# A cross attention's tail moved to tokens on rows, and its head loop given the work

## The reference, cut to what matters

```python
x = x + tanh(g_xattn[0]) * L0_xattn(layernorm(x), ctx)
x = x + tanh(g_ffn[0])   * L0_ffn(layernorm(x))
x = x + tanh(g_xattn[1]) * L1_xattn(layernorm(x), ctx, ctx, mask)
x = x + tanh(g_ffn[1])   * L1_ffn(layernorm(x))

def L1_xattn(q, k, v, mask):          # 16 heads of 16, 361 context rows
    qh, kh, vh = heads(q @ w_q.T + b_q), heads(k @ w_k.T + b_k), heads(v @ w_v.T + b_v)
    attn = softmax(where(mask, qh @ kh.T / 4, -inf))
    return merge(attn @ vh) @ w_o.T + b_o

def L1_ffn(xs):                       # 8 experts, hidden 684
    d2 = sum(xs*xs) + sum(centroid*centroid) - 2 * xs @ centroid.T
    w, sel = top_k(sqrt(maximum(d2, 1e-12)), 2); w = softmax(w)
    return sum over the two chosen e of w_e * ((silu(xs @ Wg[e] + bg[e]) * (xs @ W1[e] + b1[e])) @ W2[e] + b2[e])
```

## Time and profile before

| | |
|---|---|
| median of 3 runs | 837.34 us (836.78 to 839.22) |
| the profiled execution's own time | 836.42 us |
| its span, first to last instruction | 834.2 us |
| mean granted TensorE clock | 0.945 of full |
| busy: PE, DVE, ACT, POOL | 745.0, 562.8, 414.6, 241.5 us |
| the chain that ended last: PE, DVE, ACT, POOL | 55%, 14%, 3%, 1% |

### The profile page before, as it was taken

One profiled execution on the slowest core, in us unless ns is written; L12 is line 12 of the kernel. 1 busy time (PEld: TensorE's weight loads), 2 busy tenths in 40 slices (PEclk: granted clock), 3 DMA queues, 4 the chain that ended last, 5 costly groups with the idle time before them and its releaser, 6 DMA issues.

```text
span 834.2 us, 13705 instructions
## 1 busy us (share of the span) xinstructions
PE 745.0 (89%) x4761; PEld 621.0 (74%) x4761; DVE 562.8 (67%) x1030; ACT 414.6 (50%) x896; POOL 241.5 (29%) x195
## 2 busy tenths in 40 slices
PE   6999999999889469989998898888998699999996
PEld 3588888889865168657996566666774699999995
DVE  3369999999728979737666567676554666656652
ACT  4544444443253249835434356565664545655651
POOL 0064544444003514510003302222212133433422
PEclk9999999999999979897999899998789599999999
DMA  6400000000070000000000766545052248999972
GB/s 235 200 2 18 19 19 19 19 1 1 1 279 9 0 0 3 1 1 1 1 9 1 182 158 150 132 108 172 2 195 95 86 163 291 328 304 309 328 227 57
DMA packets 29050, 86.01 MB, mean 103 GB/s; under 512 B 3759, under 2 KB 19599, under 8 KB 25655
## 3 DMA queue, kind: packets, MB, share of 16 engines
q1 hardware_dynamic: 25143, 79.89, 29.1%
q0 software_dynamic: 3840, 5.25, 3.0%
HBM read 74.75 MB, written 10.38 MB: 102 GB/s over the span
## 4 chain that ended last, share of the span: by engine, by line
PE 55%; DVE 14%; issue 4%; ACT 3%; DMA 2%; POOL 1%; POOLq 0%; SPq 0%; DVEq 0%; ACTq 0%
PE PS L490 51%; PE PS L1033 1%; DVE SM L2049 1%; DVE WK L1811 1%; DVE RW L1751 1%; PE PS L662 1%; DVE WK L1808 1%; DMA KST<-mask_rows 1%; DVE RO L1754 1%; PE PS L879 1%; PE PS L1003 1%; ACT SQ L1078 1%; POOL OT L1565 0%; DVE M L2058 0%; DMA out<-YO,TROW 0%
## 5 line engine op out<-in xcount | busy, mean ns | idle before, releaser
L1485 POOL TENSOR_TENSOR PRODL<-RW,PRODH 128x361 fp32r<-128x361 f32 x64 | 64.8, 1016 | 114.7 <-ACT PRODH L1145 111.1
L2049 DVE TENSOR_REDUCE SM<-PS 100x1 f32<-100x362 f32 x128 | 64.9, 531 | 46.5 <-PE PS L490 45.7
L490 PE MATMUL PS<-CTXH,WKV0H 128*128 128x362 f32 x256 | 85.8, 335 | 9.5 <-DVE RW L1707 8.9
L490 PE MATMUL PS<-CTXL,WKV0H 128*128 128x362 f32 x256 | 84.1, 328 | 0.0
L490 PE MATMUL PS<-CTXH,WKV0L 128*128 128x362 f32 x256 | 83.9, 328 | 0.0
L1334 ACT ACTIVATE WK<-PS 120x400 f32<-120x400 f32 (+1 forms) x96 | 48.3, 507 | 43.1 <-PE PS L490 42.2
L490 PEld LDWEIGHTS PS<-CTXH,WKV0H 128*128 128x128 f32 x256 | 48.3, 188 | 15.9 <-DVE RW L1707 11.0
L490 PE MATMUL PS<-KST,QST 97*100 97x362 f32 x128 | 54.4, 437 | 5.9 <-DMA KST<-mask_rows 3.3
L1592 POOL DMA_INDIRECT out<-YO,TROW x20 | 31.5, 1573 | 95.2 <-PE PS L1003 45.6
L1145 ACT CAST PRODH<-RW 128x361 fp32r<-128x361 f32 x64 | 31.8, 496 | 53.7 <-DVE RW L1707 53.4
L1754 DVE TENSOR_REDUCE RO<-RW 128x100 f32<-128x400 f32 x64 | 56.1, 877 | 2.2
(11 more groups left out here) (310 smaller groups left out, 1980.8 us busy)
## 6 DMA issues: line engine op xcount, KB each, us to landing
RB<-W SPq DMA_DIRECT2D x14, 1368.0 KB, 6.0
RB<-W SPq DMA_DIRECT2D x20, 768.0 KB, 7.1
KST<-keys_by_head SPq DMA_DIRECT2D x24, 362.0 KB
RQ<-W SPq DMA_DIRECT2D x6, 1368.0 KB, 6.1
keys_by_head<-KTHL SPq DMA_DIRECT2D x8, 724.0 KB, 3.3
CTX<-ctxT SPq DMA_DIRECT2D x16, 361.0 KB, 6.6
RW<-WGU SPq DMA_DIRECT2D x1, 2304.0 KB, 8.5
RW<-WKV SPq DMA_DIRECT2D x1, 2048.0 KB, 9.9
```

Source lines behind the costliest of these rows:

```text
L490: return pe.matmul(out, lhsT, rhs, start=start, stop=stop)
L1485: pool.tensor_tensor(low, raw, high, ALU.subtract).then_inc(sem["a_products_low_ready"], 1)
L2049: dve.tensor_reduce(SM1[:, q % 2, j:j + 1], PS[0:S, i % 2, 0:KVE], AX_X, ALU.max, negate=True).then_inc(sem["c_maximum_found"], 1)
```

## The change

- **Heads packed.** WO1 has two groups of 128 full rows instead of four half empty ones. An odd group of heads takes its 32 columns of VP 16 earlier, so that its ones come first; `outs` then puts the mixtures of two groups into one set of partitions and the sums into the same, with two columns of COLS that are one on the lower or the upper half of each 32, in five steps on DVE. `divide` (DVE) multiplies by the reciprocals. The value bias is folded into the output bias by `fold_output`, and POOL's two steps are gone.
- **Output and centroid products in one.** WO1 gets eight further columns, output weights times centroids (`fold_centroids`, from WO1T, a transposed copy loaded by SP). `project_out(b)` gives for one batch, tokens on rows, 8 products with the centroids and the 256 outputs.
- **Row statistics.** `add_rows_in(b)` adds residual and its own centroid products (TOKENS = DOTS and RESID); `statistics(b)` takes mean and variance along the row; ACT makes the reciprocal deviation, `route()` builds the distances from them, and ACT writes the normed rows to ROWS, in eight steps behind the statistics.
- **Residual in the loop.** `turn_residual(i)` (PE), `copy_residual(i)` (ACT) and `dot_residual(g)` (PE) run in the loop's last two batches, after POOL has added the folded bias to X.
- **Order.** `gu_low(0, 0)` is at q == 29 of the loop, `gu_low(0, 1)` after `route()`. The five first `project_out` are in the loop's last two and a half quads.

The core of the diff:

```diff
@@ SP
             load(CENT, t["centT"], "moe1_small_loaded")
+            sp.wait_ge(sem["norm_variance_summed"], 10)
+            load(WO1T, t["WO1T"], "moe1_small_loaded")
...
             sp.wait_ge(sem["expert_weights_low_ready"], N0 + 2)
             load_weights(3)
-            sp.wait_ge(sem["rows_copied"], 4)
+            sp.wait_ge(sem["rows_copied"], B)
             sp.dma_start(XROWS.rearrange("(b s) c -> s b c", s=S), ROWS[:, :, :]).then_inc(sem["rows_stored"], 16)
-            sp.wait_ge(sem["moe_turned_copied"], 6)
+            sp.wait_ge(sem["c_rows_summed"], B)
             sp.dma_start(t["out"][0:T].rearrange("(b s) c -> s b c", s=S),
-                         RESID[:, :, :]).then_inc(sem["out_stored"], 16)
+                         RESID).then_inc(sem["out_stored"], 16)
@@ PE, in mix_v(q), behind its waits
+                if (b, g) == (4, 0):
+                    fold_output()
+                if (b, g) == (5, 0):
+                    fold_centroids()
+                if b == 6:
+                    dot_residual(g)
                 for c in range(3):
                     for j in range(4):
+                        at = 32 * (4 * g + j) - 16 * (g % 2)
                         m = mm(PS[32 * j:32 * j + 32, 6, g * S:(g + 1) * S],
-                               VP[0:CHS[c], b % 2, c, 4 * g + j, :],
+                               VPF[0:CHS[c], b % 2, c, at:at + 32],
                                PTC[0:CHS[c], q % 2, c, j * S:(j + 1) * S], c == 0, c == 2)
...
+            def fold_output():
+                pe.wait_ge(sem["c_aside_ready"], 2)
+                pe.wait_ge(sem["c_operands_ready"], 3)
+                for k in range(KD):
+                    mm(PS[:, 6, 400:408], AVG[:, :], CENT2[:, k, :], k == 0, k == KD - 1)
+                for mo in range(KD):
+                    for c in range(2):
+                        mm(PS[:, 6, 408 + mo:409 + mo], WO1[:, c, 8 + mo * P:8 + (mo + 1) * P], COLS[:, 16 + c:17 + c],
+                           c == 0, c == 1)
+                for k in range(KD):
+                    mm(PS[0:S, 6, 416:424], ONES[:, 0:S], CENTSQ[:, k, :], k == 0, k == KD - 1)
+
+            def fold_centroids():
+                pe.wait_ge(sem["router_operand_ready"], 2)
...
+                for c in range(2):
+                    for k in range(KD):
+                        mm(PS[:, 6, 400 + 8 * c:408 + 8 * c], WO1T[:, k, c * P:(c + 1) * P], CENT2[:, k, :],
+                           k == 0, k == KD - 1)
+
+            def dot_residual(g):
+                pe.wait_ge(sem["c_operands_ready"], 6)
+                for b in (2 * g, 2 * g + 1):
+                    for k in range(KD):
+                        mm(PS[0:S, 6, 400 + 8 * b:408 + 8 * b], X[:, k, tok(b)], CENT2[:, k, :], k == 0, k == KD - 1)
...
+            def project_out(b):
+                pe.wait_ge(sem["c_mixed_divided"], b + 1)
+                pe.wait_ge(sem["router_operand_ready"], 3)
...
+                for c in range(2):
+                    m = mm(PS[0:S, (0, 1, 7)[b % 3], 0:8 + D], OT1[:, c, tok(b)], WO1[:, c, :], c == 0, c == 1)
@@ PE, at the end of a quad
+                if q in (24, 28, 29, 30):
+                    turn_residual((q - 24) if q == 24 else q - 27)
+                if q in (30, 31):
+                    project_out(2 * q - 60)
+                    project_out(2 * q - 59)
@@ ACT
+                if q in (25, 29, 30, 31):
+                    copy_residual((q - 25) if q == 25 else q - 28)
...
             invert_sums(B - 1)
-            add_bias("c_output_summed", 0, 2, 1, "c_output_gated", [WK[:, i, :] for i in range(4)])
-            norm(5)
...
+            act.wait_ge(sem["c_statistics_found"], B)
+            act.activation(RSTD, MOMENTS[:, :, 1], ACT.Ln, bias=COLS[0:S, 15:16]).then_inc(sem["norm_log_taken"], 1)
+            act.wait_ge(sem["norm_log_taken"], 11)
+            act.activation(RSTD, RSTD, ACT.Exp, scale=-0.5).then_inc(sem["norm_rstd_ready"], 1)
             act.preload_act_table_set("sqrt_and_others")
...
+            for b in range(B):
+                act.activation(ROWS[:, b, :], RESID[:, b, :], ACT.Identity, bias=SHIFTS[:, b:b + 1],
+                               scale=RSTD[:, b:b + 1]).then_inc(sem["rows_copied"], 1)
@@ POOL
+            for b in range(3, B):
+                mask_queries(b)
+            pool.wait_ge(sem["router_operand_ready"], 2)
...
+            for k in range(KD):
+                pool.tensor_scalar(X[:, k, :], X[:, k, :], ASIDE[:, 8 + k:9 + k], None,
+                                   ALU.add).then_inc(sem["c_operands_ready"], 1)
@@ DVE
             def outs(b):
                 dve.wait_ge(sem["c_heads_mixed"], 4 * (b + 1))
...
+                link(dve.tensor_scalar(pair(OPPOSITE), mixed[:, :, 0, :], UPPER, None, ALU.mult))
+                link(dve.scalar_tensor_tensor(pair(OPPOSITE), mixed[:, :, 1, :], LOWER, pair(OPPOSITE), ALU.mult, ALU.add))
+                dve.stream_shuffle(SUMS, OPPOSITE, [q ^ 16 for q in range(32)]).then_inc(sem["c_mixed_copied"], 1)
+                link(dve.tensor_scalar(pair(UN), mixed[:, :, 0, :], LOWER, None, ALU.mult))
+                if b == 4:
+                    link(dve.tensor_copy(ASIDE[:, 0:10], PS[:, 6, 400:410]))
+                    dve.tensor_copy(CSQ, PS[0:S, 6, 416:424])
...
+                dve.scalar_tensor_tensor(pair(UN), mixed[:, :, 1, :], UPPER, pair(UN), ALU.mult,
+                                         ALU.add).then_inc(sem["c_mixed_copied"], 1)
...
+            def statistics(b):
+                dve.wait_ge(sem["c_rows_summed"], b + 1)
+                link(dve.bn_stats(PARTS6[:, b, :], RESID[:, b, :]))
+                dve.bn_aggr(MOMENTS[:, b, :], PARTS6[:, b, :]).then_inc(sem["c_statistics_found"], 1)
@@ DVE, the loop and behind it
+                if g == 0 and b >= 2:
+                    divide(b - 2)
                 if g == 1 and b >= 1:
                     outs(b - 1)
+                if q == 29:
+                    dve.wait_ge(sem["c_values_summed"], 2 * B)
+                    gu_low(0, 0)
...
+            for b in (0, 1):
+                add_rows_in(b)
+            for b in (0, 1):
+                statistics(b)
+            divide(B - 2)
+            for b in (2, 3):
+                add_rows_in(b)
+                statistics(b)
             outs(B - 1)
-            gu_low(0, 0)
-            gu_low(0, 1)
-            add_to_x("c_output_gated", "c_added_to_x")
-            norm(5)
+            add_rows_in(4)
+            statistics(4)
+            divide(B - 1)
+            for b in (5, 6, 7):
+                add_rows_in(b)
+                statistics(b)
...
             route()
+            gu_low(0, 1)
```

More of the change, by code:

```diff
@@ L394, in _ @@
             load(W1A, t["W1A"], "c_weights_loaded")
-            load(WO1, t["WO1"], "c_weights_loaded")
+            load(WO1[:, :, 8:8 + D], t["WO1"], "c_weights_loaded")
             for i in range(B, B + 3):
@@ new lines, in turn_residual @@
+            def turn_residual(i):
+                pe.wait_ge(sem["c_operands_ready"], 6)
+                pe.wait_ge(sem["c_values_copied"], 16 if i else 14)
+                if i:
+                    pe.wait_ge(sem["c_aside_ready"], 2 + i)
+                for x in range(2):
+                    for k in range(KD):
+                        at = (2 * x + k) * P
+                        m = pe.transpose(PS[0:S, 7, at:at + P], X[:, k, tok(2 * i + x)], IDN[:, :])
+                m.then_inc(sem["c_aside_summed"], 1)
@@ L911, in _ @@
                 ahead = q + 2 < QUADS
+                if q == QUADS:
+                    project_out(4)
                 if 0 <= q < QUADS:
@@ L1446, in _ @@
             act.preload_act_table_set("silu_and_others")
-            for i in range(4):
-                act.wait_ge(sem["moe_turned"], 6 + i + 1)
-                act.copy(RESID[:, 2 * i:2 * i + 2, :],
-                         PS[0:S, i, :].rearrange("p (x c) -> p x c", x=2)).then_inc(sem["moe_turned_copied"], 1)
             gu_high(1, 1)
@@ L2060, in split_maxima @@
                                   ALU.subtract).then_inc(sem["c_maxima_low_ready"], 1)
+            LOWER, UPPER = COLS[:, 21:22], COLS[:, 22:23]
             def outs(b):
                 dve.wait_ge(sem["c_heads_mixed"], 4 * (b + 1))
[L2064 to L2068 removed]
@@ new lines, in divide, with add_rows_in @@
+            def divide(b):
+                dve.wait_ge(sem["c_sums_inverted"], 2 * b + 2)
+                dve.wait_ge(sem["c_mixed_copied"], 2 * b + 2)
+                dve.wait_ge(sem["c_query_summed"], 4)
+                pair = lambda a: a.rearrange("p (c s) -> p c s", c=2)
+                dve.tensor_tensor(OT1[:, :, tok(b)], pair(UN), pair(SUMS), ALU.mult).then_inc(sem["c_mixed_divided"], 1)
+            def add_rows_in(b):
+                dve.wait_ge(sem["c_output_summed"], b + 1)
+                dve.wait_ge(sem["c_aside_ready"], 3 + b // 2)
+                dve.tensor_tensor(TOKENS[:, b, :], PS[0:S, (0, 1, 7)[b % 3], 0:8 + D], TOKENS[:, b, :],
```

(1 more changed line is left out.)

221 lines of the change are left out of this document (107 added, 114 removed).

## The result

| | before | after |
|---|---|---|
| median | 837.53 us | 861.28 us (858.15 to 862.90, 4 runs) |
| the profiled execution | 836.42 us | 862.76 us |
| its span | 834.2 us | 861.0 us |
| mean granted TensorE clock | 0.945 | 0.918 |

The ratio is 1.0288, 95% interval 1.0263 to 1.0313: 2.9% slower, against a forecast of 851 us (+14.5). The direction and the main mechanisms came as forecast, the size did not. The profiled execution after is one of the slower ones of the four: the medians lie 23.8 us apart, the two profiled executions 26.3 us.

The account below looks back on a forecast made before the run. PE's stop at each batch's first `mix_v` for `outs`, then the chain through the routing, bound the kernel. Loop 13 + end 6.7 - tail 17.7 + ACT 2.5 + store 10 = +14.5 on 836.4: 851 us, 8 in 10 within 840 to 861.

Parts of the forecast that it names:

- the clock in the loop: Loop: longer stops bring one or two more batches with halved PE clock, +2 us (0 to 6).
- the clock falls at every batch: Rival, loop: three further falls of 2 to 2.5 us and projections at half clock, 862 us; chance 10%.
- POOL's relief: Loop: without POOL's two steps, four DVE casts could run free (2.4 us); half taken, -1.2 us.
- Copies, narrow products, turns and projections: Loop: copies 0.8, `fold_output` 1.5, `fold_centroids` 0.7, `dot_residual` 3.3, `turn_residual` 0.5 us; at its end, projections 4.7.
- The store, +10: SP's queue: token rows' store waits behind routing and block 3's weights, delaying the gather; +10 us (+7.5 to +11.4), serial R+11.5.
- ACT, +2.5: Routing: row copies, bias cast and weight cast precede ACT's square root, for which DVE waits; +2.5 us (0 to 3.5).
- The dropped transposes of X behind the routing were beside DVE's steps: Routing on PE: removing these transposes changes nothing in time, priced at nothing.
- The tail, -17.7: Last `mix_v` to the routing arithmetic at L2124: 26.6 us becomes 8.9, -17.7 (bounds -19 and -14).
- The experts, 0: Experts behind the first token turn: an even stretch, taken to move as one block with that point.
- The products hide in PE's idle time: Rival, loop and end: idle gaps absorb PE's added work, costing 2 instead of 19.7 us; 833 us, chance 7%.
- The store isn't late: Rival, SP's queue: its wait costs nothing, leaving 4.5 us, 841 us; chance 8%.
- the signs named ahead: Stops 2.4 to 2.6 us; last `mix_v` 640 to 645; DVE's wait 2 to 3; gather 9 to 12 after routing.

Follow-up runs that it names:

- e4: The changed kernel with 8 unread fp32 products of 128 columns on PE ahead of each batch's first `mix_v`: 848.73 us, ratio 1.0154.
- e7: The kernel before with 6 unread products of 128x128 ahead of each batch's stop from the second on: 828.95 us, ratio 0.9934.
- e9: The changed kernel with SP's stores ahead of block 3's weights load and `gu_low(0,1)` moved into DVE's wait for ACT's root: 848.14 us, ratio 1.0151.
- e10: The changed kernel with e9's edits, e2's ACT order, `outs` ahead of the maxima and 4 unread products ahead of each stop: 830.90 us, ratio 0.9935.
- e12: The kernel before with `outs` ahead of the maxima on DVE and 4 unread products ahead of each stop: 826.11 us, ratio 0.9874.
- e2: The changed kernel with ACT's square root and exponential ahead of the bias cast and `gu_high(1, 0)`: 857.33 us, ratio 1.0267.
- e11: e10 with 12 unread products in PE's idle time ahead of the POSITION by NAMED products: 831.29 us, ratio 0.9942.
- e6: e10 with the 32 narrow instructions of `dot_residual` replaced by one 64-column product, so routing uses wrong distances: 828.28 us, ratio 0.9910.
- e5: The kernel before with two more linked 128x200 copies in `outs`, ahead of its second copy: 847.89 us, ratio 1.0147.
- e14: e5 with 8 unread products ahead of each stop: 838.72 us, ratio 1.0012.
- e1: The changed kernel with SP's two stores (token rows, residual) ahead of the wait and load of block 3's weights: 852.13 us, ratio 1.0183.

## Why the forecast was right, and where it failed

**The failed step is the clock in the loop.** The text said: "One more or two: +2 (0 to 6)". The count was right, six falls where there were four, but not their price. It can be worked out from the fills. e4 took out 34.2 of the change's 47.8 us at half clock and gave 12.5 us; the 13.6 that it left are worth 3.7 to 5.0 by the rates 0.27 and 0.37. e7 took out all 27.3 of the kernel before and gave 7.4. So the clock costs the change 16.2 to 17.5 us and the kernel before 7.4: the term is 8.8 to 10.1, outside its bounds. The text looked at what two more falls cost, and not at the four that were there: a fall had lasted 6.8 us on average and came to 8.0 in six, and each microsecond of it cost more in the change. The rival "the clock falls at every batch" is nearer with its 862 us, but by luck: there is no fall behind the seventh stop, and so no projections at half clock, and of the 12.3 us by which the forecast fell short in the profiled runs 4.6 lie in the store and the routing. The Trainium skill, "TensorE: Matmul & The Clock Gate", section "HAM oscillation — how this bites in real kernels", warns of a loop whose every pass holds a wait, since the fall is then paid each time instead of once. The trace agrees: seven waits of 2.6 to 3.1 us, six falls.

**Around it, in the loop.** `outs` took 2.06 us as against 1.95, and DVE's copies and differences of the folded products (0.17 to 0.23 us each) stand in three of them. But the 8.0 us of longer stops are not all lost. A batch without a fall takes 18.15 us in this loop and 17.54 before, from one shuffle to the next; e9's first batch and the first batch before:

```profile
508.15 0.37 DVE L2121 STREAM_SHUFFLE STD<-STD 128x200 f32<-128x200 f32 x1
...
526.30 0.37 DVE L2121 STREAM_SHUFFLE STD<-STD 128x200 f32<-128x200 f32 x1
```
```profile
507.54 0.60 DVE L2067 STREAM_SHUFFLE STD<-PS 128x400 f32<-128x400 f32 x1
...
525.08 0.60 DVE L2067 STREAM_SHUFFLE STD<-PS 128x400 f32<-128x400 f32 x1
```

That is 0.61 us a batch for 1.01 of stop. The rest came back, and DVE's casts show where it may come from: 8 of 26 took 0.77 to 0.95 us before, none more than 0.55 after, so POOL's relief, priced 1.2, may be up to 2.8; that all of it is POOL's was not tested. Seven times 0.61 is 4.3, and 0.9 more lie in the first `outs`, ahead of its shuffle: 5.2, where the forecast has 5.4 (6.6 - 1.2).

Copies, narrow products, turns and projections were priced at 12.3 (6.8 up to the seventh `outs` and 5.5 behind it); e10 against e12 gives 10.6 to 12.0. That is right in the sum and not one by one: the 56 narrow instructions took 6.7 us in e10, mostly at full clock, and 9.7 in the change, priced 5.5, and the end of the loop was dearer in the forecast than in the runs. From the first shuffle to the last `mix_v` the parts give 4.3 + 8.8 + 12.0 or 4.3 + 10.1 + 10.6, so 25.0 to 25.1, measured 24.8 (115.5 and 140.3). Of the other 2.05 us 0.9 are the steps ahead of the first shuffle. The remaining 1.1 were there when the first `outs` started (507.54 and 508.67); in the profiled kernels of both kinds this start lies anywhere from 503.0 to 508.8, so they can't be put to the change.

**The store, +10, measured +13.0.** Mechanism and place as forecast. The text took a value near the serial end; the gather went out at R + 12.2, where the serial end was 11.5. The store landed 10.0 us behind its issue. By the rule of the Trainium skill, "DMA: Bandwidth & Descriptors", section "Queues, rings and completion order" (descriptors are taken in ring order), the term was 11.4, and the trace sides with it, since the store side by side with the load would have had the gather at R + 7.6. What the text left out is the residual's store, called hidden because nobody waits for it. It goes out 0.4 us behind, its bytes are beside the first gather, and this took 4.3 us from issue to turn (3.7 before, 662.39 to 666.10). That the one makes the other is not shown: in e2, with the same order on SP, the gather took 3.5.

**ACT, +2.5, measured +4.1.** e2 gives 2.5 for the order on ACT, just the forecast, and the root was done 15.0 us behind the last `mix_v`, forecast 14.9. Luck is in it: the eight row copies took 4.04 us, priced 3.2, and started sooner than priced. Of the other 1.6, 1.1 lie in a part that the text priced at nothing, "The dropped transposes of X behind the routing were beside DVE's steps". They were, but the products behind them were the faster for them. PE before, and DVE's wait for it, then both after:

```profile
654.51 3.23 PE L974 MATMUL PS<-IDN,X 128*100 128x128 f32 x16
658.78 2.44 PE L490 MATMUL PS<-NAMED,POSITION 100*128 100x20 f32 x16 [1.04 <-DVE POSITION L2170]
```
```profile
661.33 0.18 DVE L2184 TENSOR_SCALAR XROW<-PS 128x20 uint32<-128x20 f32 x1 [0.27 <-PE PS L490]
```
```profile
670.35 3.59 PE L498 MATMUL PS<-NAMED,POSITION 100*128 100x20 f32 x16 [7.02 <-DVE POSITION L2268]
```
```profile
674.04 0.18 DVE L2282 TENSOR_SCALAR XROW<-PS 128x20 uint32<-128x20 f32 x1 [1.41 <-PE PS L498]
```

With 3.23 us of transposes ahead of them the 16 products took 2.44 us and DVE waited 0.27; behind 7.0 us of idle time they take 3.59 and DVE waits 1.41. e11 put work back there: 2.19 us, and no wait, but then the gather was late. The last 0.5 us of the stage stay open.

**The tail, -17.7, measured -18.2.** Right, statistics included (0.43 and 0.18 us, priced 0.42 and 0.2). These had no row of their own; that the price of another instruction fitted was luck. **The experts, 0, measured +1.1.** From the token turn to the end the profiled kernels of both kinds took 168.1 to 169.6 us, so this too can't be put to the change.

**The rivals.** "The products hide in PE's idle time" did not happen: e6 and e10 against e12 show them on the path. "The store isn't late" neither. Of the signs named ahead, four came out higher than named: the stops (2.6 to 3.1 us), the last `mix_v` (649.9), DVE's wait (3.4) and, just, the first gather (12.2 us behind R).

**What stays open.** Behind which stop the clock falls, and for how long. Stops of 2.38 us in e5 brought five falls and 31.0 us at half clock, those of 2.59 and more in the change 47.8; e2 and e9, whose loop is the change's, had five falls each, with 37.5 and 40.9 us. So one profile tells the clock's cost to some 3 us only (10 us at half clock, times 0.27 to 0.37). Why a microsecond at half clock costs 0.27 us in one kernel and 0.37 in the other is not shown. And the split of e5's 11.4 us into stop and clock rests on e14 in the loop (9.3 us less), not on e5's own tally. The change as repaired in e10 does not beat the kernel before as repaired in e12 (830.9 and 826.1). Whether it could is open: e10 still has 13.7 us at half clock and a first gather that is 1.5 us late, and a better place for the narrow products was not tried.

## What to carry to other kernels

Where an engine stands at one point of every pass, ask two prices of an edit that lengthens the stop: the stop itself, and the clock behind it. The second is read as microseconds at half clock over the whole loop, the falls that are there already included, and not from the first instruction behind a stop. A line that stays where it is in a queue can still be moved in time: follow every wait of the queue, and count the bytes of transfers that nobody waits for, because a small gather behind them does wait. And try the repair on the kernel before as well: unread products in the stop and an earlier `outs` gave it 1.3%, twice what the repaired change gains.

## What was not expected of the hardware

- Unread float32 products of 128 columns in a stop paid for themselves: 6 of them ahead of each stop took PE from 27.3 us at half clock to none in the profiled run, and the kernel from 836.5 to 829.0 us.
- The clock of an identical loop differs between executions: 47.8 us at half clock in the change and in e1, 40.9 in e9, 37.5 in e2. The skipped fall was another one each time (the third in e2, the first in e9).
- Eight instructions of 8 columns, four float32 products, took 0.79 us at full and 1.39 to 1.48 at half clock, 0.10 and 0.18 for each instruction.
- POOL's issue of the first gather took 2.80 us beside DVE's subtraction of 128x1368 (1.58 us) (e1, one gather) and 1.22 to 1.28 us without it.
- 12 unread products in front of 16 awaited ones brought these from 3.59 to 2.19 us, but 1.5 us of waiting later the next 16 took 3.60 again.
